# Expert results added to the output by accumulating scatters instead of a gathered sum at the end

## The reference, cut to what matters

```python
x = x + jnp.tanh(g_xattn[0]) * _L0_xattn_ref(ctx_2048, _layernorm(x, axis=-1), mask, mask, ...)   # x2
x = x + jnp.tanh(g_ffn[0]) * _L0_ffn_ref(_layernorm(x, axis=-1), ...)
# inside _L0_ffn_ref, x_flat being 2048 x 128:
scores = jax.nn.sigmoid((x_flat @ gate.T + bias).astype(jnp.float32))
top_scores, selected = jax.lax.top_k(scores, 2)
top_scores = top_scores / (jnp.sum(top_scores, axis=-1, keepdims=True) + EPS)
onehot = jax.nn.one_hot(selected, 9, dtype=jnp.float32)
cw = jnp.einsum('tk,tke->te', top_scores, onehot)
for e in range(9):
    h = jax.nn.silu(x_flat @ ew1[e].T) * (x_flat @ ew3[e].T)      # hidden width 352
    out = out + cw[:, e:e + 1] * (h @ ew2[e].T)
```

## Time and profile before

| | |
|---|---|
| timed runs, median (all) | 218.54 us (217.89, 218.54, 218.61) |
| profiled execution, span | 234.1 us |
| TensorE, busy share | 88% |
| VectorE, ScalarE, POOL, busy share | 64%, 61%, 55% |
| mean granted clock of TensorE | 0.968 |
| POOL's result scatters (L616) | 38, 37.8 us busy |
| POOL's row scatters (L593) | 32, 32.7 us busy |
| chain that ended last | TensorE 56%, VectorE 14%, "another core or an unknown queue" 7% |

### The profile page before, as it was taken

One profiled execution on the slowest core, in us unless ns is written; L12 is line 12 of the kernel. 1 busy time (PEld: TensorE's weight loads), 2 busy tenths in 40 slices (PEclk: granted clock), 3 DMA queues, 4 the chain that ended last, 5 costly groups with the idle time before them and its releaser, 6 DMA issues.

```text
span 234.1 us, 5788 instructions
## 1 busy us (share of the span) xinstructions
PE 205.4 (88%) x1606; PEld 166.9 (71%) x1606; DVE 149.6 (64%) x523; ACT 142.7 (61%) x399; POOL 128.8 (55%) x230
## 2 busy tenths in 40 slices
PE   8999986999999999898883946299999999999981
PEld 3577653666666676565573945299999999999881
DVE  0469997788898698897865822344443444456774
ACT  2286869988778876786471620266667666666210
POOL 4237745132325876786783578556675756557320
PEclk9999999999999999999998897589999999999998
DMA  5999999999910100011372221121222221261194
GB/s 164 368 377 242 407 381 409 408 370 318 342 55 13 36 23 26 23 36 38 86 214 62 61 76 49 41 53 55 61 69 68 52 65 47 49 218 53 37 348 163
DMA packets 23602, 34.91 MB, mean 149 GB/s; under 512 B 2562, under 2 KB 15879, under 8 KB 23443
## 3 DMA queue, kind: packets, MB, share of 16 engines
q1 hardware_dynamic: 20610, 29.27, 37.9%
q0 software_dynamic: 2240, 4.23, 5.5%
q10 hardware_dynamic: 720, 1.02, 1.5%
HBM read 15.85 MB, written 19.06 MB: 149 GB/s over the span
## 4 chain that ended last, share of the span: by engine, by line
PE 56%; DVE 14%; another core or an unknown queue 7%; ACT 6%; DMA 6%; issue 5%; POOL 4%; SPq 1%; POOLq 0%; DVEq 0%; ACTq 0%
PE pt_ps L1363 10%; PE score_ps L1321 5%; PE pt_ps L1372 4%; PE score_ps L1323 4%; PE score_ps L1322 4%; PE score_ps L1176 4%; DMA kheads<-y_rows 3%; PE pt_ps L1116 3%; PE ps_a L1226 3%; PE pt_ps L1214 3%; PE score_ps L1126 2%; PE ps_b L1283 2%; DVE less L827 2%; ACT probs L401 2%
## 5 line engine op out<-in xcount | busy, mean ns | idle before, releaser
L616 POOL DMA_INDIRECT y_rows<-vals,ids x38 | 37.8, 995 | 17.2 <-ACT vals L473 9.6
L1363 PE MATMUL pt_ps<-w,probsT 128*128 x234 | 34.4, 285 | 14.6 <-ACT probsT L480 6.7
L1363 PEld LDWEIGHTS pt_ps<-w,probsT 128*128 128x128 f32 x234 | 32.1, 198 | 15.9 <-issue 15.8
L593 POOL DMA_INDIRECT x_rows<-stage,slot x32 | 32.7, 1022 | 10.4 <-issue 7.7
L401 ACT ACTIVATE probs<-score_ps,less 128x128 f32<-128x128 f32 x128 | 37.9, 419 | 0.4 <-DVE less L827 0.4
L1043 DVE TENSOR_TENSOR xg_low<-ps_a,xg_high 128x128 fp32r<-128x128 f32 x40 | 11.7, 291 | 37.1 <-issue 23.6
L473 ACT ACTIVATE vals<-pt_ps,xg 128x128 f32<-128x128 f32 x38 | 14.0, 368 | 34.4 <-PE pt_ps L1363 24.7
L1321 PE MATMUL score_ps<-w_high,xg_low 128*128 x80 | 30.3, 379 | 0.0
L1051 DVE TENSOR_TENSOR probs<-probs,score_ps 128x352 f32<-128x352 f32 x40 | 20.8, 521 | 11.2 <-PE score_ps L1323 5.3
L1323 PE MATMUL score_ps<-w_high,xg_high 128*128 x80 | 26.6, 332 | 0.0
L1322 PE MATMUL score_ps<-w_low,xg_high 128*128 x80 | 26.5, 332 | 0.0
(11 more groups left out here) (179 smaller groups left out, 445.6 us busy)
## 6 DMA issues: line engine op xcount, KB each, us to landing
x_rows<-pads SPq DMA_DIRECT2D x1, 9945.0 KB, 37.3
w_low<-in_w13T SPq DMA_DIRECT2D x3, 1056.0 KB, 11.0
xg<-x_rows SPq DMA_DIRECT2D x40, 65.0 KB
ctx_r<-in_ctxT SPq DMA_DIRECT2D x4, 512.0 KB, 7.7
y_rows<-pads SPq DMA_DIRECT2D x1, 2048.0 KB, 16.6
w<-in_w2T SPq DMA_DIRECT2D x1, 1728.0 KB, 11.2
kheads<-y_rows SPq DMA_DIRECT2D x3, 512.0 KB, 5.0
mask_b<-in_mask SPq DMA_DIRECT2D x4, 256.0 KB, 8.0
```

Source lines behind the costliest of these rows:

```text
L593: pool.indirect_dma_start(x_rows[:, :], bass.IndirectOffsetOnAxis(ap=slot[:, par, c, p:p + 1], axis=0), stage[:, par, c, p, :], None, boun ...
L616: pool.indirect_dma_start(y_rows[:, :], bass.IndirectOffsetOnAxis(ap=ids[:, s:s + 1], axis=0), yt[:, s, :], None, bounds_check=last_row, o ...
L1363: last = nc.tensor.matmul(into[:, 0:D], hidT[:, q3, c, :], w2[:, bass.ds(e3, 1), c, :].rearrange("p o d -> p (o d)"), start=(c == 0), stop ...
```

## The change

The results are no longer kept in `y_rows`. The output tensor gets 256 more rows, which the host cuts off. x2 is stored to it in the order of the tokens, in four parts, three of them during attention (`store_x2`). POOL's scatter of a tile then adds its rows to the rows of `out` (`compute_op=ALU.add`), and all 40 tiles are scattered. An empty slot's row is added to one of the 256 extra rows. The two scatters of one token must not overlap in time. Two tiles of one expert never share a token, so tile k's scatter waits for the landing of tile k - 2's always, and for that of tile k - 1's where the expert changes or a table begins. There are two semaphores for it, `st_y`, by turns; which value to wait for is worked out by VectorE (`landed`) and loaded by POOL. All of the end behind the last result goes. VectorE writes the ids straight to `ids`, without POOL's copy, and POOL's short memsets go.

```diff
-SUMMED = 2
-BY_DVE, BY_POOL, BY_PE, ALL_PE = (0, 1), 2, 3, 4
+TURNS = 2
+FIRSTS = [sum(TILES[:n]) for n in range(len(TILES))]
...
+        def scattered(t):
+            return t // TURNS * 16 + 16
...  (SP)
-            sp.dma_start(y_rows.rearrange("(p n) d -> p n d", p=P), pads[:, 0:1, 0:D].to_broadcast([P, 2 * NB, D])).then_inc(st_zero, 16)
+            sp.dma_start(out[NB * P:(NB + TURNS) * P].rearrange("(n p) d -> p n d", p=P), pads[:, 0:TURNS, 0:D]).then_inc(st_zero, 16)
+            def store_x2(g):
+                here = slice(g * UN, (g + 1) * UN)
+                sp.wait_ge(x2_done, (g + 1) * UN * 2 - 1)
+                sp.dma_start(out[0:NB * P].rearrange("(b t) d -> t b d", b=NB)[:, here, :], xs[:, here, :]).then_inc(x2_stored[g], 16)
+            for g in range(NG - 1):
+                store_x2(g)
             for n in range(len(EARLY)):
                 if n == 1:
-                    sp.wait_ge(x2_done, NB * 2 - 1)
-                    sp.dma_start(out.rearrange("b t d -> t b d"), xs[:]).then_inc(x2_stored, 16)
+                    store_x2(NG - 1)
...
-            sp.dma_start(xs[:], out_tok).then_inc(x2_back, 16)
-            for place in range(YR):
-                sp.wait_ge(st_y[place], len(range(place, NT - SUMMED, YR)) * 16)
...
+            for n in range(TURNS):
+                sp.wait_ge(st_y[n], scattered(NT - TURNS + n))
...  (ScalarE, before a result is written)
                     if t >= YR:
-                        act.wait_ge(st_y[t % YR], t // YR * 16)
+                        act.wait_ge(st_y[t % TURNS], scattered(t - YR))
...  (POOL)
-            def tile(k, r):
-                s = k % YR
-                pool.wait_ge(ids_cast, k + 1)
-                if k >= YR:
-                    pool.wait_ge(st_y[s], k // YR * 16)
-                nc.gpsimd.tensor_tensor(ids[:, s:s + 1], ids_in[:, s:s + 1], zero[:], ALU.add).then_inc(ids_copied, 1)
-                pool.wait_ge(ids_copied, k + 1)
+            def tile(k):
+                s, turn = k % YR, k % TURNS
+                if k in FIRSTS or k <= TURNS:
+                    if k >= 1:
+                        pool.wait_ge(st_y[(k - 1) % TURNS], scattered(k - 1))
+                else:
+                    if k - 1 in FIRSTS or k == TURNS + 1:
+                        pool.wait_ge(landed_known, sum(f < k for f in FIRSTS))
+                    pool.wait_ge(st_y[(k - 1) % TURNS], pool.value_load(landed[0:1, k:k + 1], min_val=16, max_val=16 * NT))
+                    pool.sem_inc(rows_apart, 1)
                 if k == 0:
                     pool.wait_ge(st_zero, 16)
-                if k < 3 * TR:
-                    short_space()
+                    for g in range(NG):
+                        pool.wait_ge(x2_stored[g], 16)
+                if k >= TURNS:
+                    pool.wait_ge(st_y[turn], scattered(k - TURNS))
+                pool.wait_ge(ids_cast, k + 1)
                 pool.wait_ge(y_done, k + 1)
-                pool.indirect_dma_start(y_rows[:, :], bass.IndirectOffsetOnAxis(ap=ids[:, s:s + 1], axis=0), yt[:, s, :], None,
-                                        bounds_check=last_row, oob_is_err=False).then_inc(st_y[s], 16)
+                pool.indirect_dma_start(out[:, :], bass.IndirectOffsetOnAxis(ap=ids[:, s:s + 1], axis=0), yt[:, s, :], None,
+                                        bounds_check=last_row, oob_is_err=True, compute_op=ALU.add).then_inc(st_y[turn], 16)
...
-            for k in range(NT - SUMMED):
-                tile(k, k % TR)
+            for k in range(NT):
+                tile(k)
...  (VectorE, in table_rows)
+                nc.vector.tensor_tensor(changed[:, 1:tiles], expert_f[:, 1:tiles], expert_f[:, 0:tiles - 1], ALU.not_equal)
+                nc.vector.scalar_tensor_tensor(landed[:, at + 1:at + tiles], changed[:, 1:tiles], 16.0, part["landed"][0:1, at + 1:at + tiles],
+                                               ALU.mult, ALU.add).then_inc(landed_known, 1)
...  (VectorE, cast_ids)
-                    dve.wait_ge(ids_copied, t + 1 - YR)
-                nc.vector.tensor_copy(ids_in[:, t % YR:t % YR + 1], xg[:, place, C_ID:C_ID + 1]).then_inc(ids_cast, 1)
+                    dve.wait_ge(st_y[t % TURNS], scattered(t - YR))
+                nc.vector.tensor_scalar(ids[:, t % YR:t % YR + 1], xg[:, place, C_ID:C_ID + 1], part["nowhere"][:, t % TURNS:t % TURNS + 1], None,
+                                        ALU.min).then_inc(ids_cast, 1)
...
-            for u in range(NB // UN):
-                choose_rows(u, 1)
```

More of the change, by code:

```diff
@@ L61, with build @@
 FIRST = {"ident": P, "head_rows": HH, "gates": 2, "b_key": 1, "b_qry": 1, "b_val": D}
-CONSTS = {"mask_t": NB, "b_res": D, "rows_below": P, "experts": NE, "first_rows": NE, "first_ids": 2 * UN, "nowhere": 1, "gate_b": NE, "rows_of": P, "blocks": NB}
-ROW_CONSTS = {"first_tiles": NE, "experts_upto": NE * NE, "tiles": NT, "digits": NT}
+CONSTS = {"mask_t": NB, "b_res": D, "rows_below": P, "experts": NE, "first_rows": NE, "first_ids": 2 * UN, "nowhere": TURNS, "gate_b": NE}
+ROW_CONSTS = {"first_tiles": NE, "experts_upto": NE * NE, "tiles": NT, "digits": NT, "landed": NT}
 ROUNDER = 1.5 * 2.0 ** 23
 NCTX, WARM = 3, 24
-def build(nc, x, ctxT, mask, first, consts, row_consts, w_srcT, w_tgtT, w_outT, w13T, w2T, gateT, x_rows, y_rows, out):
+def build(nc, x, ctxT, mask, first, consts, row_consts, w_srcT, w_tgtT, w_outT, w13T, w2T, gateT, x_rows, out):
     with ExitStack() as ctx:
@@ L136, in build @@
         pads = sb("pads", [P, NE, RW])
-        ids_in = sb("ids_in", [P, YR], I32)
-        xg, xg_high, xg_low, ids, zero = sb("xg", [P, TR, RW]), sb("xg_high", [P, 2, P], F32R), sb("xg_low", [P, 2, P], F32R), sb("ids", [P, YR], I32), sb("zero", [P, 1], I32)
+        changed, landed = sb("changed", [1, NT]), sb("landed", [1, NT], I32)
+        xg, xg_high, xg_low, ids = sb("xg", [P, TR, RW]), sb("xg_high", [P, 2, P], F32R), sb("xg_low", [P, 2, P], F32R), sb("ids", [P, YR], I32)
         flat = [t[:].rearrange("p a h t -> p (a h t)") for t in (probs, probsT)]
@@ L174, in build @@
         st_last = [sem(f"st_last{n}") for n in range(UN)]
-        st_y = [sem(f"st_y{n}") for n in range(YR)]
-        ld_y = [sem(f"ld_y{n}") for n in range(len(PARTS))]
-        x2_stored, x2_back, st_out = sem("x2_stored"), sem("x2_back"), sem("st_out")
+        st_y = [sem(f"st_y{n}") for n in range(TURNS)]
+        x2_stored, landed_known, rows_apart = [sem(f"x2_stored{n}") for n in range(NG)], sem("landed_known"), sem("rows_apart")
         dve_chain, act_chain, pool_set, table_chain = sem("dve_chain"), sem("act_chain"), sem("pool_set"), sem("table_chain")
@@ L520, in _ @@
             pool.wait_ge(ld_rest, 16)
-            nc.gpsimd.tensor_copy(pads[:, :, C_ID], part["nowhere"].to_broadcast([P, NE])).then_inc(pad_set, 1)
+            nc.gpsimd.memset(pads[:, :, C_ID:C_ID + 1], float(NOWHERE)).then_inc(pad_set, 1)
             rstd(1)
@@ L631, in _ @@
                         scatter(NG - 1, p)
[L633 to L636, removed]
         @block.vector
@@ L806, in weigh @@
                                                ALU.mult, ALU.mult).then_inc(weighed, 1)
-                nc.vector.tensor_scalar(stage[:, g % 2, :, :, C_ID], part["first_ids"].rearrange("p (c b) -> p c b", c=2), 2.0 * UN * P * g, None, ALU.add)
+                nc.vector.tensor_scalar(stage[:, g % 2, :, :, C_ID], part["first_ids"].rearrange("p (c b) -> p c b", c=2), float(UN * P * g), None, ALU.add)
                 assert route_links["weigh"] == LINKS["weigh"]
@@ L975, in _ @@
             table_counts(1)
[L977 to L981, removed]
-                dve.wait_ge(token_known, 1)
-                nc.vector.tensor_scalar(token[:], token[:], ROUNDER, ROUNDER, ALU.add, ALU.subtract).then_inc(token_known, 1)
-                dve.wait_ge(token_known, 2)
-                nc.vector.tensor_tensor(apart[:], token[:].unsqueeze(2).to_broadcast([P, SUMMED, NB]), part["blocks"].unsqueeze(1).to_broadcast([P, SUMMED, NB]),
-                                        ALU.subtract).then_inc(token_known, 1)
-                dve.wait_ge(token_known, 3)
-            def choose_rows(u, n):
-                here = slice(u * UN, (u + 1) * UN)
-                nc.vector.tensor_tensor(chosen_rows[:, n, here], part["rows_of"].unsqueeze(1).to_broadcast([P, UN, P]),
-                                        apart[:, n, here].unsqueeze(2).to_broadcast([P, UN, P]), ALU.is_equal).then_inc(row_chosen, 1)
             def cast_ids(t, place, turn):
@@ L1438 @@
         "first_rows": np.arange(NE) * CAP,
-        "first_ids": (np.arange(UN) * 2 * P + np.arange(2)[:, None]).reshape(1, -1) + np.arange(P)[:, None] * 2,
-        "nowhere": NOWHERE + np.arange(P)[:, None],
-        "rows_of": NB * np.arange(P),
-        "blocks": np.arange(NB),
+        "first_ids": np.tile(np.arange(UN) * P, 2) + np.arange(P)[:, None],
+        "nowhere": np.arange(NB, NB + TURNS) * P + np.arange(P)[:, None],
```

(7 more changed lines are left out.)

102 lines of the change are left out of this document (7 added, 95 removed).

## The result

The changed kernel takes 272.25 us (median of four runs, 271.29 to 275.13) against 218.21 us (216.7 to 218.61) for the kernel before: a ratio of 1.2502, 95% interval 1.242 to 1.2585. The forecast was 234 us, 221 to 253. The direction was right and the mechanism too; the price of one step of that mechanism was far too low.

What follows compares the result with a forecast made beforehand. POOL's chain of scatter landings was to set the end: 139.9 us, plus 69.0 for 23 waiting steps and 21.7 for 14 others, landing at 233.2, plus 0.9, gives 234.1 us; range 221 to 253 us.

Steps and rivals of the forecast that it cites:

- The stalls: Five pieces between tiles 0 and 5 with engines standing still, 16.45 us, taken to belong to the profiled execution alone.
- Tile 2's start: On POOL's queue, tile 2's result scatter was to start at 139.9 us, after the row scatters.
- 23 waiting and 14 other steps: POOL's scatters from tile 2 on: 23 wait for the one just before, 69.0 us; 14 do not, 21.7 us.
- the ring of results: The results' 16 places for ScalarE and VectorE were to hold, so that tiles do not stall.
- the price of a waiting step: From one POOL scatter's start through its landing to the next start: 3.0 us, between 2.53 and 4.27.
- The landing: From an accumulating scatter's start to its landing: 2.6 us, between 2.13 and 3.87.
- the reaction: From a landing to the next scatter's start on POOL: 0.40 us.
- A step that does not wait: On POOL, a scatter, its issue and the wait value's load: 1.55 us, between 1.30 and 1.85.
- The load of the value: POOL's new load of the wait's value, about 0.53 us, which might or might not hide behind the scatter.
- The end: Behind tile 39's scatter start at 230.6 us, only its landing at 233.2, plus 0.9 us.
- The second: In the accumulating scatter, the read stands wholly before the write: landing 3.87 us, 268.8 us; chance 0.12 including all over 252.
- The third: POOL keeps pace with the tiles, under 2.04 us a step in the mean: faster, 207.3 us; chance 0.08.

Runs made afterwards that it cites:

- apart: Changed kernel with second choices' results in rows of their own and no waits between scatters, additions in the DMA kept, second choices not added to returned blocks: 218.62 us.
- x2_groups: Kernel before with only x2 stored in four groups, three of them during attention: 218.1 us, ratio 1.0003.
- plain: Changed kernel with the addition taken out of the DMA, so scatters overwrite rows, all waits kept: 241.1 us, ratio 1.1065.
- const16: Changed kernel with the first two tables' waits between scatters written as constants, the third table keeping the register: 267.38 us, ratio 1.2161.
- allconst: Changed kernel with all 23 waits written as constants at the steps these inputs' routing gives, no value loaded: 259.81 us, ratio 1.1888.
- wait_alone: Kernel before with each result scatter, not adding, waiting on a constant for the landing of the one ahead: 271.57 us, ratio 1.246.
- apart_plain: Changed kernel with second choices' results in rows of their own, no waits between scatters and no addition in the DMA: 214.02 us, ratio 0.982.

## Why the prediction was right in kind and wrong in size

**What held.** POOL's queue sets the end and the new waits are the cause (apart, 53.6 us). The stalls did belong to one execution (x2_groups' span of 217.0 against 234.1 - 16.45 = 217.65). Tile 2's start, and the 23 waiting and 14 other steps, came as counted. The stores of x2 cost nothing, and the ring of results, though it fills, cost nothing either. From tile 17 on the scatters come in pairs.

**The step that failed: the price of a waiting step,** 3.0 us forecast, bounds 2.53 to 4.27, and 4.18 us measured in the mean ((261.68 - 139.65 - 14 x 1.85) / 23). Both of its terms were too small. The landing alone would have stayed within the range: with 3.3 us the forecast's own sum gives 139.9 + 23 x 3.7 + 21.7 + 3.3 + 0.9 = 250.9 us. What carries the time out of it is the reaction, 11 us, which stood at 0.40 us at both ends of the bounds, as if it were certain, and the smaller terms below, 10 us.

- The landing, 2.6 us, measured 3.3: 23 x 0.7 = 16 us. The forecast set it a quarter of the way from a plain landing to one with a whole load added; it lies near two thirds. The lower end, 2.13, was an empty tile's scatter (plain, 2.25). The forecast reasoned on the memory side alone, whether the reads can overlap. More than half of the addition's 1.07 us, 0.57, is on POOL before the first packet moves: a scatter of 144 packets for one of 32 (plain against the changed kernel).
  By the Trainium skill, "Collectives: The Full Stack" ("Why ReduceScatter is half of AllGather"), only the second read would count, an estimate of 2.28 us; by its "DMA: Bandwidth & Descriptors", under latency, a round trip of 0.8 us, an estimate of 2.93. The runs agree with neither: 3.3, the nearer one being the dearer. The Trainium skill's "DMA: Bandwidth & Descriptors" ("SWDGE vs HWDGE vs iDMA") says that DMAs issued from GpSimd have their descriptors computed by software, which fits POOL's 1.54 us for 144 packets against 0.97 for 32.
- The reaction, 0.40 us, measured 0.88: 23 x 0.48 = 11 us. It was read in the earlier trace rows at a scatter that carried its wait itself, and POOL had been idle for only 0.27 us before that scatter. In the changed kernel an instruction of its own does the waiting, so the DMA's dispatch of 0.7 us, which used to lie under the wait, comes behind the landing. const16 and allconst give 0.6 us of it back; wait_alone shows nearly the same price, 0.77 us in all, with a constant. Where the scatter itself waits, 0.27 us are left.

**The smaller terms.** A step that does not wait was put at 1.55 us and takes 1.85: +4 us. The load of the value, over which the forecast was in doubt, is hidden; POOL's own 1.54 us are the reason. The end was taken as a landing, 2.6 us, and is POOL's scatter and DRAIN, 7.7 us: +5; the DRAIN stood in the trace of before, level with the end, and the forecast did not price it. Around the span lie 1.9 us (271.29 - 269.4), not 0.9: +1. Together 27.1 + 4.2 + 5.1 + 1.0 - 0.25 = 37.2 us on 234.1: 271.3 us, the profiled run's 271.29. This sum closes by construction, since the 4.18 us is worked out from the last scatter's start.

**The rivals.** The second, at 268.8 us, is near the measured time, but not for its reason: it had the landing at 3.87 and the reaction at 0.40. The third gave 2.04 us a step as the point where it turns faster. apart took 1.85 us a step and came out even; with 7.7 + 1.9 us at the end the point is near (218.4 - 9.6 - 139.65) / 37 = 1.87 us.

No kernel here that computes the whole is faster than the kernel before; a wait carried by the DMA saves some 12 us of the 54 (allconst). The only faster one, apart_plain, leaves the additions out, and what it gains, 4.6 us, would have to pay for them. What stays open is how the 0.5 us in the transfer divide between the reading of rows and the number of packets; no run separates them, and the pages of plain and of the changed kernel count the same 12.63 MB read from HBM, so the reading of the rows does not show there at all.

## What to carry to other kernels

Price a chain in which each DMA waits for the one before by its whole period: the engine's time to write the transfer, the transfer, the confirmation, and the dispatch of the next. Read the last from a place where the wait stands as it will stand, since a wait ahead of the DMA uncovers the dispatch and one that the DMA carries does not (0.75 to 0.9 us from landing to start here, against 0.27). Before counting a removed tail as gain, look for what else ends near it: here POOL's DRAIN, which already ended level with the tail.

## What the runs showed of the hardware

- An accumulating scatter of 128 rows of 512 B is 144 packets, where a plain one is 32 (the changed kernel against plain). It keeps POOL for 1.54 us instead of 0.97, and lands in 3.3 us instead of 2.25.
- POOL's DRAIN at the end of the program ended 5.95 to 6.0 us after its last scatter in the changed kernel (269.2), apart_plain (210.2) and plain: there the last scatter is off POOL at 231.24 and the span is 237.4. In the kernel before it ended 5.8 us after POOL's last addition (228.04 and 233.8).
- Accumulating scatters without waits between them followed at POOL's pace, 1.85 us (apart).
- From the landing that a result scatter waits for to its start on POOL lay 0.27 us where the scatter itself waits (allconst), and 0.75 to 0.78 us (wait_alone) or 0.9 us (changed kernel, plain) where an instruction ahead of it does.
